# Attention pipeline on one core: layer norm moved into the preceding step's last group, projections and splits into the first, scratch laid out in 4 KB rows, side work placed at other units

## The reference

```python
x = x + 0.5 * moe(layernorm(x), Wr, We)     # 8 experts, top 2
x = x + attention(layernorm(x), Wq, bq, Wk, bk, Wv, bv, Wo, bo)
x = x + 0.5 * moe(layernorm(x), Wr, We)

# attention: 16 heads of 8 features
scores = einsum('bthd,bshd->bhts', q, k) / sqrt(8) + alibi      # -slope * |t - s|
scores = where(s > t, -inf, scores)
out = softmax(scores) @ v @ Wo + bo
```

## Time and profile before

| | us |
|---|---|
| median of 3 runs | 1023.84 |
| lowest and highest run | 1015.57, 1025.05 |
| the profiled execution's own time | 1020.61 |
| span of its profile, first to last instruction | 1018.9 |
| busy PE / DVE / ACT / POOL | 869.3 / 756.3 / 634.8 / 537.1 |
| mean granted TensorE clock over the span | 0.893 of full |

### The profile page before, as it was taken

One profiled execution on the slowest core, in us unless ns is written; L12 is line 12 of the kernel. 1 busy time (PEld: TensorE's weight loads), 2 busy tenths in 40 slices (PEclk: granted clock), 3 DMA queues, 4 the chain that ended last, 5 costly groups with the idle time before them and its releaser, 6 DMA issues. The chain is left out here.

```text
span 1018.9 us, 24637 instructions
## 1 busy us (share of the span) xinstructions
PE 869.3 (85%) x6498; PEld 396.8 (39%) x6498; DVE 756.3 (74%) x2534; ACT 634.8 (62%) x1538; POOL 537.1 (53%) x838
## 2 busy tenths in 40 slices
PE   4989995389798897898998988989989995998997
PEld 3444442143243343433433433433433433544443
DVE  5999984477776777778777777778777813799996
ACT  4676764007665575676676666666766783676765
POOL 3777775234453553544544544535535231677777
PEclk9999997557897898989988988988988997899999
DMA  6600000653644725535526436346247000011001
GB/s 170 95 0 0 0 0 1 155 120 77 116 98 70 147 61 96 132 66 112 121 67 122 105 68 137 89 81 140 76 80 155 2 2 22 11 31 31 27 25 42
DMA packets 92532, 75.15 MB, mean 74 GB/s; under 512 B 11540, under 2 KB 92308, under 8 KB 92308
## 3 DMA queue, kind: packets, MB, share of 16 engines
q1 hardware_dynamic: 92488, 74.63, 34.8%
HBM read 44.97 MB, written 29.36 MB: 73 GB/s over the span
## 5 line engine op out<-in xcount | busy, mean ns | idle before, releaser
L1099 DVE TENSOR_REDUCE att_neg_max<-att_max 128x1 bf16<-128x512 f32 (+3 forms) x704 | 416.3, 637 | 149.3 <-PE att_max L893 147.3
L992 ACT ACTIVATE att_probs<-att_exp 128x512 f32<-128x512 f32 x640 | 352.5, 600 | 201.2 <-PE att_exp L912 196.8
L1064 POOL TENSOR_SCALAR_AFFINE_SELECT att_probs<-att_probs 128x512 f32<-128x512 f32 x256 | 157.7, 638 | 272.1 <-ACT att_probs L992 272.1
L890 PE MATMUL att_max<-att_k_max,att_q_st 51*128 51x384 bf16 (+2 forms) x768 | 198.9, 304 | 56.4 <-DMA att_k_exp<-qk_parts 48.2
L912 PE MATMUL att_exp<-att_q_st,att_k_exp 64*128 64x512 bf16 (+3 forms) x1024 | 230.2, 326 | 4.8 <-DMA att_q_st<-att_shift 3.3
L928 PE MATMUL att_pv<-att_probs,att_v 128*32 128x512 f32 (+3 forms) x2048 | 216.2, 498 | 1.5 <-POOL att_probs L1064 1.5
L358 ACT ACTIVATE moe_scaled<-moe_hi,moe_gates 128x128 f32<-128x128 f32 x512 | 146.1, 372 | 60.6 <-PE moe_hi L304 60.3
L893 PE MATMUL att_max<-att_k_max,att_q_st 62*128 62x128 bf16 x1024 | 182.1, 233 | 0.0
L518 DVE SCALAR_TENSOR_TENSOR x<-moe_lo,moe_gates,x 128x128 f32 (+1 forms) x512 | 160.5, 338 | 19.5 <-PE moe_lo L298 18.4
L890 PEld LDWEIGHTS att_max<-att_k_max,att_q_st 51*128 51x128 bf16 x768 | 74.1, 99 | 253.8 <-DVE att_neg_max L1099 164.4
L298 PE MATMUL moe_lo<-moe_we,moe_hT 128*128 128x512 f32 x256 | 136.0, 614 | 0.0
(11 more groups left out here) (81 smaller groups left out, 892.2 us busy)
## 6 DMA issues: line engine op xcount, KB each, us to landing
qk_parts<-att_parts SPq DMA_DIRECT2D x192, 128.0 KB, 2.4
att_q_st<-qk_parts SPq DMA_DIRECT2D x64, 192.0 KB, 3.8
att_k_max<-qk_parts SPq DMA_DIRECT2D x64, 192.0 KB, 5.0
att_k_exp<-qk_parts SPq DMA_DIRECT2D x64, 192.0 KB, 6.1
x<-in_L_attn_x SPq DMA_DIRECT2D x16, 256.0 KB, 3.1
out<-x SPq DMA_DIRECT2D x16, 256.0 KB, 2.3
moe_we<-in_L_ffn_We SPq DMA_DIRECT2D x2, 512.0 KB, 4.6
att_q_st<-att_shift SPq DMA_DIRECT2D x64, 4.0 KB, 4.0
```

The lines of the kernel that those rows point to most:

```text
L890: nc.tensor.matmul(max_ps[m % RING][:, at:at + width - P], q_st[par][low:low + FINE_ROW, r, i * P:(i + 1) * P], k_max[par][low:low + FINE_ ...
L992: nc.scalar.activation(probs[g % 2][:, n, :], exp_ps[m % RING][:], ACT.Exp).then_inc(exp_done, 1)
L1064: nc.gpsimd.affine_select(out=view, in_=view, compare_op=ALU.is_ge, fill=0.0, base=0, pattern=[[0, 4], [1, P]], channel_multiplier=-1).the ...
L1099: nc.vector.tensor_reduce(neg_max[par][:, g // 2, 1 - g % 2, heads[0]:heads[0] + len(heads), i], max_ps[m % RING][:, 0:len(heads) * width] ...
```

## The change

The two tables are written anew. Statistics, root, shift and the four `normalise` parts move from group 0 of step b (for sequence b+2) to group 3 of step b (for sequence b+3); `turn_h` moves to (0,3), `project_q` to (0,7), `project_k` to (1,0), the splits to (0,10) and (1,0) to (1,6). `shift_hi` moves from (0,2) to (1,5), `shift_lo` from (2,3) to (2,7), `turn_o1` from (1,3) to (1,9), `turn_o` from (2,0) to (2,3), `project_v` from (2,6) to (3,0), `output` from (3,1) to (3,4), `turn_o0` from (3,3) to (3,9), and the bias addition from (3,4) to (2,4). A step b = -3 is added so that the layer norm of sequence 0 has a last group to be in, and two more steps are written out rather than looped.

The scratch is laid out anew: before, one part of one head's feature is a row of 1 KB (512 bf16), and the rows of one head pair lie together; after, the eight head pairs of one feature lie side by side, so that a half's four pairs are 4 KB in one piece. The access patterns of stores and stacks change with it. The order of SP's DMAs, their number and the bytes that they move stay as they are, and so do all compute instructions.

```diff
--- before.py
+++ after.py
@@ -562,15 +562,17 @@
 
 
 SIDE_WORK = [
-    {2: "shift_hi"},
-    {1: "turn_h", 3: "turn_o1", 5: "project_q", 8: "project_k"},
-    {0: "turn_o", 3: "shift_lo", 6: "project_v"},
-    {1: "output", 3: "turn_o0"},
+    {3: "turn_h", 7: "project_q"},
+    {0: "project_k", 5: "shift_hi", 9: "turn_o1"},
+    {3: "turn_o", 7: "shift_lo"},
+    {0: "project_v", 4: "output", 9: "turn_o0"},
 ]
 
-PREPARE = {(0, 1): "statistics", (0, 2): "aggregate", (0, 3): "add_eps", (0, 4): "take_root", (0, 6): "shift_mean",
-           (0, 7): "normalise0", (0, 8): "normalise1", (0, 9): "normalise2", (0, 10): "normalise3", (1, 6): "split_q0", (1, 7): "split_q1", (1, 8): "split_q2", (1, 9): "split_q3",
-           (1, 10): "split_k0", (2, 0): "split_k1", (2, 1): "split_k2", (2, 2): "split_k3", (3, 4): "add_bias"}
+
+PREPARE = {(0, 10): "split_q0", (1, 0): "split_q1", (1, 1): "split_q2", (1, 2): "split_q3",
+           (1, 3): "split_k0", (1, 4): "split_k1", (1, 5): "split_k2", (1, 6): "split_k3", (2, 4): "add_bias",
+           (3, 0): "statistics", (3, 1): "aggregate", (3, 2): "add_eps", (3, 3): "take_root", (3, 6): "shift_mean",
+           (3, 7): "normalise0", (3, 8): "normalise1", (3, 9): "normalise2", (3, 10): "normalise3"}
 PV_AFTER = {3: 0, 5: 1, 7: 2, 9: 3}
 MAX_UNITS = 11
 EXP_UNITS = 10
@@ -657,7 +659,7 @@
 
 
 
-    scratch = nc.dram_tensor("qk_parts", [2, 2, PAIRS, 2, len(Q_PARTS), HD, S], BF16, kind="Internal").ap()
+    scratch = nc.dram_tensor("qk_parts", [2, 2, len(Q_PARTS), 2, HD, PAIRS, S], BF16, kind="Internal").ap()
     w, q_st, k_max, k_exp, v = ops.w, ops.q_st, ops.k_max, ops.k_exp, ops.v
     bq_col, bk_col, bv_col, bo_rows = ops.bq_col, ops.bk_col, ops.bv_col, ops.bo_rows
     with ExitStack() as ctx:
@@ -763,12 +765,12 @@
 
         def all_steps(eng, step):
 
-            for b in range(-2, 2):
+            for b in range(-3, 2):
                 step(b, b % 2, b // 2)
-            with eng.Fori(1, NSEQ // 2 - 1) as i:
+            with eng.Fori(1, NSEQ // 2 - 2) as i:
                 step(2 * i, 0, i)
                 step(2 * i + 1, 1, i)
-            for b in range(NSEQ - 2, NSEQ + 1):
+            for b in range(NSEQ - 4, NSEQ + 1):
                 step(b, b % 2, b // 2)
 
         def there(b):
@@ -782,8 +784,11 @@
                         on_max(b + 1, 1 - par, half + par, g, n)
                     if on_exp and n < EXP_UNITS and there(b):
                         on_exp(b, par, half, g, n)
-                    if on_prepare and (g, n) in PREPARE and there(b + 2):
-                        on_prepare(b + 2, par, half + 1, PREPARE[g, n])
+                    if on_prepare and (g, n) in PREPARE:
+                        if g < GROUPS - 1 and there(b + 2):
+                            on_prepare(b + 2, par, half + 1, PREPARE[g, n])
+                        if g == GROUPS - 1 and there(b + 3):
+                            on_prepare(b + 3, 1 - par, half + par + 1, PREPARE[g, n])
                     if on_side and n in SIDE_WORK[g] and present(b, SIDE_WORK[g][n]):
                         on_side(b, par, half, SIDE_WORK[g][n])
                     if on_pv and n in PV_AFTER:
@@ -827,7 +832,7 @@
                 for term in sorted(range(len(which)), key=lambda t: which[t]):
                     part = which[term]
                     sp.wait_ge(split_step[side], b * 4 + (1, 3, 4)[part])
-                    sp.dma_start(scratch[par, side, :, :, term].rearrange("r u d s -> (r u) d s"),
+                    sp.dma_start(scratch[par, side, term].rearrange("u d r s -> r (u d) s"),
                                  parts[side][:, part]).then_inc(scratch_in[par][side], DMA)
 
             def stack(b, par, half, hf):
@@ -842,7 +847,7 @@
                     for dst in stacks:
                         for ab in range(2):
                             sp.dma_start(dst[par][ab * SIDE:ab * SIDE + HEAD_ROWS, pairs, :],
-                                         scratch[par, side, pairs, ab].rearrange("r t d s -> (t d) r s")).then_inc(
+                                         scratch[par, side, :, ab, :, pairs]).then_inc(
                                 stack_in[par][hf], DMA)
 
             def place_shift(b, par, half, hf):
```

## The result

The changed kernel measured 1027.88 us in the median of 20 runs (1021.95 to 1041.48), the kernel before 1022.26 us in as many (1013.09 to 1026.88). The ratio of the two is 1.007, with a 95% interval of 1.0039 to 1.01. So it is slower by seven tenths of a percent, which lies inside the 1% that we had set as "no change". The forecast was 1065 us, 4% slower; the measured time is inside the range of 955 to 1125, but the size of the forecast's slowdown is not what happened.

A forecast was written before the change was run, and what follows sets the result against it. The DMA chain split, store, stack, maxima bounds the kernel: 15.8 + 11.5 + 1.9 + 11.5 + 1.5 = 42.2 us a step against 39.6, +36 us over 14 steps, +5 at start-up: 1065 us, range 955 to 1125.

The forecast's parts named there:

- start-up: Before step -1: nothing hides the first stack, 13.0 against 8.7 us, plus about 1 us for stores; +5 us.
- What bounds the kernel: Steps of 39.6 us: closed by a chain split, store, stack, maxima, with PE and DVE nearly as long.
- what the compute body becomes: Compute of one step: falls from 38.8 to 34.5 us as waits and part of the slow clock go.
- The item on POOL: POOL's splits and masks before the products at (2,3): costs nothing, or half a microsecond a step.
- SP's order: SP's queue: q stores stand behind the second half's shift DMAs; first store 14.1 to 15.8 us into the step.
- The engine counts: DMAs of the new layout: 8 engines carry a store and 6 a stack, where both had 16.
- The prices of the packets: Stores and stack: 60 ns per 1 KB store packet, 240 ns per 4 KB stack packet; 11.5 us each phase.
- The first rival: Transfers come in time, chain 34.6 us, body decides: 955 us; chance 0.24 with a half-way form of 1000 us.
- The signs: Profile after: 8 and 6 completion packets, first store at 14 to 16 us, PE waits 5 us+, group 0 clock under 1.
- The end doesn't move: Whole kernel: prices between, a stack wait as long as today's, 1014 to 1034 us; chance 0.10.
- The rival of the other side: Steps: stores and stack together under 20.4 us, so the body decides, 954 us; chance 0.24 with its half-way form.
- The compute wait at (2,0): PE at (2,0) waits for the late shift_hi: up to 1 us per step, 14 us; 969 us, inside the 0.24.

The follow-up runs named there:

- old_rows: The changed kernel with the scratch layout and access patterns of before (1 KB rows, 16 engines), tables as changed: 949.08 us, ratio 0.9368 to the kernel before.
- thin_stack: The changed kernel with each stack DMA from the third sequence on moving 8 partitions instead of 48, operands stale: 958.45 us in one run.
- late_k: Changed tables with the scratch layout of before, and split_k2 moved to (1,10), split_k3 to (2,0): 932.19 us, ratio 0.916 to the kernel before.
- shift_between: The changed kernel with SP issuing the second half's two shift DMAs between q and k stores, not ahead of both: 957.9 us, ratio 0.9429.
- rows4k_16: The changed kernel with each stack DMA reading 48 rows of 4 KB at one constant stride, 16 engines, operands permuted: 949.99 us, ratio 0.9333.
- rows1k_6: Changed tables, 1 KB rows as before, but each stack DMA reads 6 x 32 rows, 6 engines, operands permuted: 1015.97 us, ratio 0.9974.
- late_k_between: Changed tables, layout of before, split_k2 at (1,10), split_k3 at (2,0), second half's shift DMAs between q and k stores: 929.1 us, ratio 0.9127.

## Why the prediction was wrong in size and right in its mechanism

The step that failed is the price of the packets in the term for stores and stack: 60 ns for a store's packet and 240 ns for one of the stack's, where the runs show 51 and 196. The steps of the sum in the order of the prediction, with means over eleven steps of the changed kernel's trace:

| term | forecast | measured |
|---|---|---|
| body of a step, seen in old_rows and thin_stack | 34.5 | 34.7, 34.8 |
| step's start to the first store | 15.8 | 15.7 |
| stores, and their landing | 11.5 + 1.9 = 13.4 | 8.1 + 3.4 = 11.5 |
| stack to the next step's start | 11.5 + 1.5 = 13.0 | 12.4 |
| chain = step | 42.2 | 39.6 |
| start-up | +5 | +6.8 |

*What bounds the kernel* and *what the compute body becomes* held. The DMA chain bounded the steps before as well, and the body came out 0.2 us from the forecast. That closeness is partly luck. The forecast of 34.5 us had next to nothing for POOL's masks; with the wait for them taken away, late_k shows a body of 32.9 us. So the forecast of PE and DVE was 1.6 us too long, and the masks' wait with its slow clock filled that up. The item on POOL held only in part: "nothing, or half a microsecond a step" was 1.05 us a step (14.9 us over 14), and the clock fell behind it in six of the 14 steps of old_rows. The allowance for it had been worked out to 0.4 us on a path of 10 us, too fine for such a sum.

*SP's order* held: the first store goes out 15.7 us into the step, behind the two shift DMAs, and shift_between shows that taking this wait away is enough to make the change a gain.

*The engine counts* held, 8 and 6, though no row before had a count under 14, and rows4k_16 and rows1k_6 show that they set the stack's time. The rule of the Trainium skill ("DMA: Bandwidth & Descriptors", the section on why a DMA increments its semaphore by 16) gives just these two numbers, and the 3456 missing completion packets agree with it.

*The prices of the packets* are the step that failed. I took the store's packet at 60 ns, since it was "the same kind of packet from the same partitions". In the changed kernel it is 0.442 x 16 x 11 us / 1536 = 51 ns. The price had been read where 16 engines were at work. The first rival had named why that is too dear ("fewer engines in each other's way"), and the packet table above bears it out for the stack: part of what is lost in the number of engines comes back in speed. Why a packet is quicker then isn't shown. The stores take 12 x 16 x 51 ns = 9.8 us instead of 11.5, which with a landing of 1.7 is the measured 11.5. For the stack I took 240 ns for 4 KB, by scaling; measured are 0.328 x 16 x 12.2 / 327 = 196 ns (the share counts the completion packets' time as well; the table's 189 doesn't), nearer to the 178 ns of the best slice: 48 x 196 ns = 9.4 us instead of 11.5. That the stack's term nevertheless was only 0.6 us off is luck, an error on the other side: beside the packets' time the stack needs 3.0 us, not 1.5. Its data begin 1.5 us after the first issue, and the next step starts 1.5 us behind the last packet. The kernel before had 0.9 and 1.8 us for the same two, so most of this was mis-sized from the start: the 1.5 left only 0.6 for completion and the first tile. The packets were priced 3.8 us too high and the latencies 1.3 us too low, net 2.5 us in a chain of 42, or 6%. Against a step of 39.6 they are nearly the whole of the slowdown that was forecast, +36 us over 14 steps. The chain's sum was right to 6% and the difference that it was made for was wrong altogether: where two lengths of 40 us are subtracted, a price known to 20% is not enough to give the sign.

*The signs.* Three of those named came: the completion packets, the first store, the granted clock under 1 in group 0. The fourth, a wait of 5 us or more where each step begins, did not: 54.9 us in 15 pieces are 3.7 us each.

*The chances* followed from the mid price. "The end doesn't move" had 0.10, with the mechanism that came true (a stack wait about as long as today's). The bounds of the two prices gave chains of 34.6 to 50.4 us around a break-even at 39.6; with that spread this case deserved more, and the forecast less than 0.60.

*The rival of the other side* (the body decides, 954 us) is what each of four kernels shows as soon as one link is shortened: 949, 958, 958 and 950 us. Its deciding point was given as 20.4 us for stores and stack without their latencies. The changed kernel lies just on that point, with 9.8 + 9.4 = 19.2 us and 1.3 us more of latency.

*The compute wait at (2,0)* for the late `shift_hi` does not appear in old_rows (1.0 us in all). In the changed kernel PE's waits for a shift row sum up to 2.1 us in the whole span. It is real all the same: where the order edit moves the shift DMAs back, it comes to 23.7 us (shift_between) and 11.8 us (late_k_between).

## What to carry to other kernels

Look at the outermost count of both sides of a DMA before the length of its rows: a rearrangement that makes rows four times longer, but leaves 8 or 6 as the outermost count, takes half or more of the engines away and can cost more than all that the rows give. In a pipeline closed by a chain through an in-order queue, write the chain and the body as two lengths; whatever shortens the shorter one is worth nothing, and a wait at the head of the queue is as costly as a slow transfer. And when the two lengths are near each other, say so as two cases with equal chances, instead of pricing the difference.

## What the runs showed of the hardware beyond what was expected

- The time for which SP is busy with issuing a stack DMA hardly followed the number of its rows: the median pair for half 0 took 0.89 us with 16 engines and 48 rows of 4 KB (rows4k_16), 0.93 with 16 engines and 192 rows of 1 KB (old_rows), but 1.41 with 6 engines and 48 rows (changed kernel) and 1.56 with 6 engines and 192 rows (rows1k_6). It isn't a rule of the number of engines alone: the median store took 0.57 us with 8 engines (changed kernel) and 0.60 with 16 (old_rows), and a pair of thin_stack's DMAs of 8 rows 0.63.
- Packets of a stack, of equal rows and bytes, took 189 ns with 6 engines and 291 ns with 16 (4 KB), and 53 ns and 87 ns (1 KB). Six engines thus did the work of sixteen in 9.3 us instead of 6.0 (from the first packet to the last, 4 KB), not in 16/6 of the time.
- 4 KB rows over 16 engines were hardly faster than 1 KB rows over 16: 8.4 us from first issue to use, against 8.4 and 9.3.
- A wait of PE of 0.9 us went with the lower clock level in some steps and not in others of the same kernel (0.92 and 0.90 us, granted clock of the group 0.83 and 1.00 in old_rows). With the wait away (late_k) the group had 1.00 in all steps.
